# Splitting the attention scores of the feed-forward stage into two halves, and dropping one GpSimd addition

## The reference

```python
q = (src @ Wq).reshape(Bb, Tt, H, DH).transpose(0, 2, 1, 3)
k = (src @ Wk_c @ Wk).reshape(Bb, Tt, H, DH).transpose(0, 2, 1, 3)
v = (src @ Wv_c @ Wv).reshape(Bb, Tt, H, DH).transpose(0, 2, 1, 3)
...
attn = jnp.einsum('bhqd,bhkd->bhqk', q, k) / np.sqrt(DH).astype(np.float32)
attn = jax.nn.softmax(attn, axis=-1)
sa = jnp.einsum('bhqk,bhkd->bhqd', attn, v)
sa = sa.transpose(0, 2, 1, 3).reshape(Bb, Tt, C) @ Wo
x = _rmsnorm(src + sa, norm1_w)
```

## Time and profile before

| | us |
|---|---|
| median of 3 runs | 3362.94 (3358.84 to 3366.79) |
| the profiled execution, its own time | 3363.22 |
| span of its trace | 3361.2 |
| maximum of block 0 starts | 2762.94 |
| maximum of block 3 starts | 2798.60 |
| maximum of block 7 starts | 2837.08 |
| the next stage starts | 2890.4 |

### The profile page before, as it was taken

One profiled execution on the slowest core, in us unless ns is written; L12 is line 12 of the kernel. 1 busy time (PEld: TensorE's weight loads), 2 busy tenths in 40 slices (PEclk: granted clock), 3 DMA queues, 4 the chain that ended last, 5 costly groups with the idle time before them and its releaser, 6 DMA issues. The chain is left out here.

```text
span 3361.2 us, 50813 instructions
## 1 busy us (share of the span) xinstructions
PE 3135.3 (93%) x18068; PEld 2664.4 (79%) x18068; DVE 2480.7 (74%) x3447; ACT 1728.2 (51%) x3283; POOL 1744.6 (52%) x1122
## 2 busy tenths in 40 slices
PE   5999999999999999999999996988989877899996
PEld 4788888888888888888888885867767655678996
DVE  4699999999999999999999996685675754523213
ACT  3466666666666666666666663253453426211000
POOL 4365665566556566566555664141441436346663
PEclk9999999999999999999999997989999889899998
DMA  5544444454454445444454444100000120123220
GB/s 195 157 119 111 117 116 113 117 129 98 120 123 121 114 105 127 109 123 115 102 129 117 113 101 116 57 28 28 1 16 1 58 62 1 63 70 125 83 88 32
DMA packets 216084, 312.41 MB, mean 93 GB/s; under 512 B 28704, under 2 KB 122016, under 8 KB 207648
## 3 DMA queue, kind: packets, MB, share of 16 engines
q1 hardware_dynamic: 213024, 300.74, 34.3%
q0 software_dynamic: 2816, 8.46, 0.7%
HBM read 151.75 MB, written 23.13 MB: 52 GB/s over the span
## 5 line engine op out<-in xcount | busy, mean ns | idle before, releaser
L480 POOL TENSOR_TENSOR es<-es,e 128x512 f32<-128x512 f32 x480 | 621.7, 1295 | 741.6 <-ACT e L556 741.6
L645 DVE TENSOR_TENSOR e_hl<-e,e_hl 128x512 fp32r<-128x512 f32 x512 | 679.7, 1327 | 0.3 <-ACT e L556 0.3
L489 POOL TENSOR_TENSOR c_lo<-raw,c_hi 128x512 fp32r<-128x512 f32 x248 | 427.0, 1722 | 0.0
L636 DVE TENSOR_SCALAR sc<-ps_s,top 128x512 f32<-128x512 f32 x512 | 384.6, 751 | 55.7 <-ACT e L556 1.4
L715 PEld LDWEIGHTS ps_s<-q_hl,k_hl 128*128 128x128 f32 x2048 | 308.6, 190 | 67.7 <-issue 28.5
L632 DVE TENSOR_TENSOR ps_s<-ps_s,right 128x512 f32<-128x512 f32 x512 | 353.4, 690 | 9.1 <-ACT right L565 7.8
L715 PE MATMUL ps_s<-q_hl,k_hl 128*128 128x256 f32 x2048 | 330.9, 284 | 15.4 <-DVE sc L636 15.4
L665 PE MATMUL ps_p<-c_hi,wa 128*128 128x512 f32 x1024 | 339.1, 392 | 4.5 <-PEq L115 4.5
L665 PE MATMUL ps_p<-wa,c_hi 128*128 128x512 f32 x1024 | 337.8, 391 | 0.0
L676 PE MATMUL ps_o<-e_hl,v_hl 128*128 128x256 f32 x2048 | 331.1, 284 | 3.3 <-DVE e_hl L645 3.3
L552 ACT ACTIVATE e_hl<-sc 128x512 fp32r<-128x512 f32 x512 | 324.7, 634 | 1.4 <-PE ps_o L676 1.0
(11 more groups left out here) (395 smaller groups left out, 7371.7 us busy)
## 6 DMA issues: line engine op xcount, KB each, us to landing
k_hl<-ot SPq DMA_DIRECT2D x1024, 128.0 KB, 2.8
raw<-in_ctx_t SPq DMA_DIRECT2D x64, 1024.0 KB, 6.4
raw<-in_L_ffn_W_experts SPq DMA_DIRECT2D x64, 256.0 KB, 2.9
q_hl<-q_hi_scratch SPq DMA_DIRECT2D x32, 256.0 KB, 5.5
q_hl<-q_lo_scratch SPq DMA_DIRECT2D x32, 256.0 KB, 6.3
raw<-in_L_xattn_Wkv SPq DMA_DIRECT2D x8, 512.0 KB, 4.9
q_hi_scratch<-qa_qh SPq DMA_DIRECT2D x16, 256.0 KB, 2.5
q_lo_scratch<-qa_ql SPq DMA_DIRECT2D x16, 256.0 KB, 3.4
```

The source lines that it names most:

```text
L480: g.tensor_tensor(ES[:, GL], ES[:, GL], e, ALU.add).then_inc(summed, 1)
L489: g.tensor_tensor(C_lo[:, n % 2, k, :], RAW[:, n % 2, k, :], C_hi[:, n % 2, k, :].bitcast(F32), ALU.subtract).then_inc(clo_done, 1)
L636: v.tensor_scalar(SC[:, s % 2].rearrange("p (j q) -> p j q", j=GRP), halves[:, :, 0, :], top[:, i * (M // P) + kt16:i * (M // P) + kt16 + ...
L645: v.tensor_tensor(E2[:, s % 2, :, 1, :], E[:, s % 2].rearrange("p (j q) -> p j q", j=GRP), E2[:, s % 2, :, 0, :].bitcast(F32), ALU.subtrac ...
```

## The change

Steps of the four engines are split into two halves, hf = 0 and 1. Half 0 holds the heads in PSUM banks 0 and 1 (h % 4 of 0 or 1), half 1 those in banks 2 and 3. Each half has its own group of 8 score products, its own maximum over 1024 elements with its own negation, and its own 8 exponentials. The second addition of GpSimd is gone, and the sum on VectorE reads 64 numbers a head (1024) instead of 32 (512). Counters of semaphores follow. The order of lists becomes:

- TensorE: transposes 0 and 1, scores of half 0, transpose 2, scores of half 1, transpose 3, PV, projection. Scores of half 0 wait for the first 8 exponentials of the block before.
- ScalarE: copies 0 and 1, exponentials of half 0, copies 2 and 3, exponentials of half 1, `OT_hi`.
- VectorE: maximum and negation of half 0, the same of half 1, then as before.

```diff
             for b in range(B):
...
                 g.tensor_tensor(SS[:], w_[:, :, 0:P // 2], w_[:, :, P // 2:], ALU.add).then_inc(halved, 1)
-                g.wait_ge(halved, 2 * b + 1)
-                g.tensor_tensor(SS[:, :, 0:P // 4], SS[:, :, 0:P // 4], SS[:, :, P // 4:], ALU.add).then_inc(halved, 1)
-
                 g.wait_ge(rec_done, b + 1)
...
+                for hf in range(2):
+                    if at(k - 2):
+                        b = k - 2
+                        for n in (2 * hf, 2 * hf + 1):
+                            a.wait_ge(p_turned, 4 * b + n + 1)
+                            if b:
+                                a.wait_ge(pv_done, b)
+                            a.copy(flat(PT[:, 4 * n:4 * n + 4]), bank(5 - n % 2)).then_inc(pt_copied, 1)
+                    if at(k):
+                        a.wait_ge(maxed, 4 * k + 2 * hf + 2)
...
+                        for h in range(hf * HH, (hf + 1) * HH):
+                            a.activation(S[k % 3][:, h], ps[:, h * P:(h + 1) * P], ACT.Exp, scale=HF ** -0.5,
+                                         bias=mx[:, k % 2, h:h + 1]).then_inc(s_expd, 1)
...
+                for hf in range(2):
+                    if at(k):
+                        m_ = mx[:, k % 2, hf * HH:(hf + 1) * HH]
+                        v.wait_ge(s_done, 2 * k + hf + 1)
+                        v.tensor_reduce(m_, ps[:, hf * HH * P:(hf + 1) * HH * P].rearrange("p (h f) -> p h f", f=P), AX.X, ALU.max).then_inc(maxed, 1)
+                        v.wait_ge(maxed, 4 * k + 2 * hf + 1)
+                        v.tensor_scalar(m_, m_, -HF ** -0.5, None, ALU.mult).then_inc(maxed, 1)
                 if at(k - 1):
                     b = k - 1
-                    v.wait_ge(halved, 2 * (b + 1))
-                    v.tensor_reduce(sm[:, b % 2], SS[:, :, 0:P // 4], AX.X, ALU.add).then_inc(summed, 1)
+                    v.wait_ge(halved, b + 1)
+                    v.tensor_reduce(sm[:, b % 2], SS[:], AX.X, ALU.add).then_inc(summed, 1)
...
+                for hf in range(2):
+                    if at(k - 2):
+                        turn_weights(k - 2, 2 * hf)
+                        if hf == 0:
+                            turn_weights(k - 2, 1)
+                    if at(k):
+                        if k:
+                            t_.wait_ge(s_expd, H * (k - 1) + HH * (hf + 1))
+                        for h in range(H):
+                            if h % 4 // 2 == hf:
+                                q_ = slice(h % 4 * HF, (h % 4 + 1) * HF)
+                                mm = t_.matmul(bank(h % 4)[:, h // 4 * P:(h // 4 + 1) * P], QT[q_, h // 4, k * P:(k + 1) * P],
+                                               KT_[q_, h // 4, k * P:(k + 1) * P], start=True, stop=True)
+                        mm.then_inc(s_done, 1)
...
                 if at(k - 2):
                     b = k - 2
-                    turn_weights(b, 2)
                     turn_weights(b, 3)
```

More of the change, by code:

```diff
@@ L1523, in stage_ffn_attend @@
         BEHIND = 3
+        HH = H // 2
         NU = len(UNITS)
@@ L1585, in _ @@
             for k in STEPS:
[L1586 to L1601, removed]
+                for hf in range(2):
[8 more added lines that the diff above has]
+                        a.wait_ge(maxed, 4 * k + 2 * hf + 2)
+                        if k == 1:
+                            a.wait_ge(wq_lo_done, 2)
+                        if k >= 3:
+                            a.wait_ge(p_turned, 4 * (k - 2))
+                        for h in range(hf * HH, (hf + 1) * HH):
+                            a.activation(S[k % 3][:, h], ps[:, h * P:(h + 1) * P], ACT.Exp, scale=HF ** -0.5,
+                                         bias=mx[:, k % 2, h:h + 1]).then_inc(s_expd, 1)
                 for b in VALUES.get(k, ()):
```

## The result

The changed kernel takes 3376.68 us (median of 7 runs, 3373.73 to 3379.98), the kernel before 3362.68 (7 runs, 3358.73 to 3366.79). The ratio is 1.0042, with a 95% interval of 1.003 to 1.0053: slower by 10 to 18 us, 14.0 by the medians of the two.

The account below looks back on a forecast made before the run. The step's loop through VectorE, ScalarE's exponentials and `OT_hi` (9.62 us) was taken as the bound, growing to 11.72 through PV and projection. +8.4 + 1.6 - 2.0 + 8.5 = +16.5 on 3363.2 gave about 3380 us, range 3365 to 3388.

Parts of the forecast that it names:

- the sum of +16.5: Whole kernel: loop +8.4, step 8 on +1.6, start-up -2.0, clock +8.5, added to the profiled 3363.2 us.
- scores of block 0 to maximum of block 3: Start-up: scores of block 1 start after 8 exponentials, transposes of step 2 at 2781.4 instead of 2783.40; -2.0 us.
- four steps, loop and clock: Maximum of block 3 to that of block 7: longer loop +8.4 us, half clock 1.7 us a step.
- maximum of block 7 to the next stage: Step 8's transposes start at the projection's end, 8.68 instead of 7.12 after the maximum: +1.6, with 1.7 for clock.
- The loop: Steady steps: copies 2 and 3 behind exponentials delay PV, projection, `OT_hi` and the next maximum; 11.72 us against 9.62.
- GpSimd's loop: Steady steps, transposes through maximum, sum, reciprocal and scaling: 10.47 us, shorter than the deciding loop; 9.65 with fast halves.
- The clock: TensorE idles 3.3 us each step and falls to half clock in two steps of three: 5 x 1.7 = +8.5 us.
- The start-up: Steps 0 to 2: negations held by GpSimd, but scores of block 1 start sooner; -2.0 us, bounds -5.9 and +0.4.
- The halves: Maxima and scores: a 1024-element reduction takes 1.22 us, a half's scores 1.10, as long as the whole.
- 0.9 more of VectorE's work a step: VectorE's list: two maxima of 1.22 us with a second negation, and a sum 0.54 longer, add about 0.9.
- The second addition: GpSimd: dropping its 1.26 us inside the wait for the reciprocal gains steady steps nothing; up to 1.3 in step 8.
- The rival on the other side: PV and projection fit before `OT_hi`, GpSimd's loop decides at 9.65: -6.6 us, 3356.6; chance 0.06.

Follow-up runs that it names:

- the order alone: Kernel before, with only ScalarE's copies 2 and 3 of turned weights moved behind the first 8 exponentials: 3384.2 us, ratio 1.007.
- the copies first and TensorE kept at work: Changed kernel, all four copies ahead of both exponential groups, extra matmuls in TensorE's wait for the scaling: 3364.1 us, ratio 1.0014 to the kernel before.
- the two runs with extra matmuls in the steady steps: Changed kernel with thrown-away matmuls between fourth transpose and PV: 3369.7 us; changed kernel with all copies first and matmuls in the wait for the scaling: 3364.1 us.
- the projection first: Changed kernel, with the projection of block k-3 moved ahead of PV in TensorE's list: 3372.7 us, ratio 1.0037 to the kernel before.
- the copies first: Changed kernel, with all four copies of turned weights ahead of both exponential groups in ScalarE's list: 3372.9 us, ratio 1.004 to the kernel before.

## Why the prediction was right

3380 was forecast, between 3365 and 3388; 3376.7 was measured. That the two are so close is in part luck: against the stretch the sum of +16.5 was 1.6 too low, against the medians 2.5 too high, and the errors of its terms partly cancel. The mechanism was the one forecast. Point by point, against the stretch of the profiled executions:

| term | forecast | measured |
|---|---|---|
| scores of block 0 to maximum of block 3 | -2.0 | -1.35 (35.55 against 36.90) |
| four steps, loop and clock | +8.4 + 6.8 = +15.2 | +16.95 (55.43 against 38.48) |
| maximum of block 7 to the next stage | +1.6 + 1.7 = +3.3 | +2.5 (55.91 against 53.39) |
| sum | +16.5 | +18.1; by the medians +14.0 |

*The loop.* Shown. Its sum of 11.72 was met by 11.77 at full clock; its releasers stand in the waits; the order alone on the old kernel brings it about. Taking either of its two links away (the copies behind exponentials, the projection behind PV) broke the loop in the traces, but won nothing clear by the totals: slow transposes and scores on GpSimd's loop kept the step at 12. With the copies first and TensorE kept at work 10.1 of the 14.0 us were won back by the medians.

*The clock.* Shown as a cost on the path by the two runs with extra matmuls in the steady steps. The size was 2.1 a step (13.86 less 11.72), between my 1.7 and the 2.6 of a slow spell in every step. I had it in two steps of three; the windows show every step below 1.00. Step 5 of the changed kernel, TensorE:

```profile
2826.11 1.08 PE L1763 MATMUL g_ps<-g_pt,g_v 128*32 128x128 f32 x32 [3.46 <-ACT g_pt L1590]
2827.12 0.78 PE L1684 MATMUL g_ps<-wa,g_ot_lo 128*128 128x512 f32 x1
```

The Trainium skill's page TensorE: Matmul & The Clock Gate, section HAM oscillation, tells of a loop that starts every burst at the low clock. The trace agrees in part: in steps 4 and 6 PV was slow (1.94), in steps 5 and 7 it ran at full clock (1.08) and only the projection behind it was slow, so the fall did not always come before the burst, but every step lost some.

*The start-up.* Its -2.0 was there where it was forecast: the transposes of step 2 start 19.63 after the scores of block 0 (2777.37 less 2757.74), before 21.70. Before the maximum of block 3 some 0.7 came back, 0.54 of it the longer sum (1.21 against 0.68), which my start-up left out.

*The halves.* The price of a half's scores was 1.09 at full clock (2805.30 to 2806.39, 16 passes), of a reduction 1.22 and 1.21. Both were as taken. GpSimd's loop of 10.47 was 10.6 when it could be seen, with some 0.2 of it from the extra matmuls. The forecast's 0.9 more of VectorE's work a step should have been 0.8 by its own terms (2 x 1.34 less 2.41, and 0.54), and nothing hung on it.

*The second addition* was worth nothing, as forecast; dropping it alone, with the longer sum, is a small loss. Before that run I had it at 1 us at most, it is 4, because I left the clock out of that loop.

*The rival on the other side* needed the projection to end before 6.5 after the maximum; in the step shown the transposes behind it start 10.7 after it (2834.79 to 2845.52), and at full clock, in the run with extra matmuls between the transposes and PV, 8.6 (2813.63 to 2822.21).

*What stays open.* The stretch grew by 18.1 in one execution, the medians by 14.0. With the projection first and with the copies first it is the other way round (10.2 and 10.6 against 12.9 and 13.1). Whether the clock falls more or less often in other executions can't be told from one trace of each kernel.

## What to carry to other kernels

Splitting a step so that its first half starts sooner moves something else back in an engine's list: follow who waits for the work behind the new place, through every engine, and add up that loop, before counting what starts sooner. When a wait of TensorE grows, add what the work behind it costs at half clock, and look at which loop that work is on; here cheap work in the wait was worth more than work removed elsewhere. A part that is dropped inside another engine's wait is worth nothing, and what replaces it may not be free.

## What the hardware showed that I had not expected

TensorE's clock also fell in steps whose idle stretches were well under 3 us. Behind 1.95, 1.96 and 2.23 us of idleness the scores ran at half speed (of half a block 2.08 against 1.16, of a whole block 2.09 against 1.17). The 8 transposes ahead of them took 1.79 and 1.84 behind 1.96 and 2.23, but 1.27 behind 1.95, against 1.09. Behind 1.50, 1.58 and 1.78 all ran at full. These are single steps, and other waits in the same steps differ too, so they bound nothing more than themselves.

An operation on VectorE over 8 or 16 numbers (the negation, 0.17 us alone) did not end before GpSimd's elementwise operation beside it: it took 2.79, 3.97 and, in step 1 of the changed kernel, 2.00, each time ending within 0.03 of that operation. The reductions next to it were not held, though GpSimd ran beside them, and neither was the moments' pass over `rows` (L88): 0.69 beside GpSimd's first addition (2836.07 in the kernel before) and 0.69 with GpSimd idle (2853.47). ScalarE did the same negation beside GpSimd in 0.22.
